# The late x work moves into light steps and the tail gets longer distances, in a graph network kernel on Trainium2

## What is computed

```python
agg = jax.ops.segment_sum(edge_attr, col, num_segments=x.shape[0])
h = jnp.concatenate([x, agg, u[batch]], axis=1)
h = jax.nn.relu(h @ W1 + b1)
out = h @ W2 + b2
x = _layernorm(x + (out + x))
```

## Time and profile before

| | us |
|---|---|
| median of 3 runs | 185.68 (185.62 to 186.27) |
| profiled execution, its own time | 185.73 |
| its span, first to last instruction | 184.0 |
| PE busy | 154.1 (84%) |
| VectorE busy | 115.4 (63%) |
| ScalarE busy | 51.5 (28%) |
| GpSimd busy | 25.4 (14%) |

### The profile page before, as it was taken

How to read it: one execution, slowest core, us unless ns; L and a number is a source line. 1 busy time by engine, 2 the same in 40 slices (tenths; PEclk the granted TensorE clock), 3 DMA queues, 4 the chain that set the end, 5 groups by cost and what they waited for, 6 DMA issues and landing times.

```text
span 184.0 us, 5378 instructions
## 1 busy us (share of the span) xinstructions
PE 154.1 (84%) x2195; PEld 113.9 (62%) x2195; DVE 115.4 (63%) x369; ACT 51.5 (28%) x110; POOL 25.4 (14%) x29
## 2 busy tenths in 40 slices
PE   0056979979979979969979999899889799899970
PEld 0046855955955956845846858467458568677850
DVE  6847499568376385485495466954933745877371
ACT  2021233223323313313313343133133241233230
POOL 7800030110200200200200204002003230000000
PEclk9999999999999999999999999999999999999997
DMA  5999999999999999999999999999999999998011
GB/s 119 315 352 373 374 375 373 371 373 374 374 374 373 375 372 373 376 372 373 374 373 374 375 373 374 375 373 360 363 374 374 371 374 370 367 398 303 11 43 33
DMA packets 42196, 62.07 MB, mean 337 GB/s; under 512 B 1975, under 2 KB 39541, under 8 KB 42170
## 3 DMA queue, kind: packets, MB, share of 16 engines
q1 hardware_dynamic: 41046, 61.23, 95.0%
q10 hardware_dynamic: 1124, 0.48, 1.2%
HBM read 58.50 MB, written 3.20 MB: 335 GB/s over the span
## 4 chain that ended last, share of the span: by engine, by line
PE 44%; DMA 39%; SPq 8%; DVE 4%; ACT 1%; issue 1%; DVEq 0%
DMA edge_ring<-in_edge_attr_dram 37%; PE sum_ps L845 17%; PE turn_ps L867 7%; PE hid_ps L907 6%; PE hid_ps L900 6%; PE out_ps L920 5%; SPq L276 4%; SPq L291 3%; DMA base_row<-in_dst_dram 2%; DVE bases L568 2%; PE xt_ps L920 1%; PE xt_ps L882 1%; DVE local_rows L576 1%; ACT local_t L429 1%; PE xt_ps L834 1%
## 5 line engine op out<-in xcount | busy, mean ns | idle before, releaser
L845 PE MATMUL sum_ps<-edge_ring,onehot 128*32 128x128 f32 x1662 | 58.5, 284 | 13.0 <-DMA edge_ring<-in_edge_attr_dram 10.8
L845 PEld LDWEIGHTS sum_ps<-edge_ring,onehot 128*32 128x32 f32 x1662 | 45.2, 113 | 27.9 <-DMA edge_ring<-in_edge_attr_dram 13.3
L630 DVE TENSOR_TENSOR agg_t<-agg_t,turn_ps 128x128 f32 x70 | 20.2, 288 | 56.7 <-PE turn_ps L867 52.6
L594 DVE TENSOR_TENSOR onehot<-iota,local_t 128x768 f32<-128x768 f32 (+1 forms) x40 | 33.6, 843 | 3.0 <-ACT local_t L429 2.4
L402 POOL TENSOR_TENSOR x_all<-x_all,half_b 128x512 f32<-128x512 f32 (+3 forms) x16 | 17.7, 1115 | 127.4 <-PE xt_ps L882 127.4
L466 ACT ACTIVATE hid_t<-hid_ps,bias 128x512 f32<-128x512 f32 (+3 forms) x32 | 18.1, 584 | 37.1 <-PE hid_ps L907 37.1
L867 PE MATMUL turn_ps<-place,sums 128*128 128x128 f32 (+1 forms) x140 | 26.5, 306 | 0.0
L907 PE MATMUL hid_ps<-agg_t,w_a 128*128 128x512 f32 (+3 forms) x64 | 24.1, 500 | 0.6 <-DVE agg_t L630 0.5
L867 PEld LDWEIGHTS turn_ps<-place,sums 128*128 128x128 f32 (+1 forms) x140 | 18.9, 192 | 8.0 <-issue 7.9
L920 PE MATMUL out_ps<-w_sb,hid_t 128*128 128x128 f32 (+1 forms) x176 | 21.9, 275 | 0.0
L441 ACT COPY sums<-sum_ps 128x256 f32<-128x256 f32 (+2 forms) x40 | 13.6, 341 | 25.9 <-PE sum_ps L845 25.9
(11 more groups left out here) (64 smaller groups left out, 73.0 us busy)
## 6 DMA issues: line engine op xcount, KB each, us to landing
edge_ring<-in_edge_attr_dram SPq DMA_DIRECT2D x69, 768.0 KB, 12.1
x_all<-in_x_dram SPq DMA_DIRECT2D x10, 256.0 KB, 10.5
out_dram<-x_all SPq DMA_DIRECT2D x1, 2304.0 KB
dst_rows<-in_dst_dram SPq DMA_DIRECT2D x1, 384.0 KB
x_all<-in_x_dram SPq DMA_DIRECT2D x1, 384.0 KB, 11.1
out_dram<-x_all SPq DMA_DIRECT2D x3, 128.0 KB
out_dram<-x_all SPq DMA_DIRECT2D x1, 256.0 KB
w_x<-in_L_gnn_W_dram ACTq DMA_DIRECT2D x1, 128.0 KB, 5.9
```

Source lines behind the costliest of these rows:

```text
L594: nc.vector.tensor_tensor(onehot[0:ROWS, b % BUFFERS, 0:k * TILES], cols, loc, ALU.is_equal).then_inc(onehot_ready, 1)
L630: nc.vector.tensor_tensor(to, to, turn_ps[b % 2][:, i * SPAN:(i + 1) * SPAN], ALU.add).then_inc(group_added, 1)
L845: last = nc.tensor.matmul(bank[c * WIN:(c + 1) * WIN], onehot[0:p, b % BUFFERS, i * TILES + c * R + r], edge_ring[0:p, slot, c * R + r], s ...
```

## The change

Node pieces: the last three are now ODD (106 nodes), E and END (128 each), so that END, a whole tile, is last. Groups 60 to 65 are handled in pairs; singles begin at group 66, which makes 37 batches. The step tables cover all pieces, and no engine has an order by hand any more. In the order of the diff:

- x of the last six pieces is loaded at groups 2, 5 and 9 (`late_load_at`) and transposed in the steps 5, 8 and 11, steps without a block's hidden or output product (`light_step`: 5, 8, 11, 14, 17, 22, 25, 28). In steps 8, 11, 14 and 17 PE multiplies the turned x of A to ODD with the x half of W1 (`sum_x_chunk`, into `out_ps`), and ScalarE keeps the result in `x_hid_late`.
- For A to ODD PE later makes the aggregate half alone, VectorE adds the kept x half (`add_x_hidden`), and ScalarE takes ReLU from the sum.
- The x half of blocks 1 to 5 and 7 to 9 is made one step earlier than the aggregate half (`hidden_x_step`).
- In the tail the output product comes two steps after the hidden one (`OUT_LATER`), the moments one step behind that, and the scaling two steps behind the moments. VectorE scales all pieces (`pool_scaled` is empty).
- `agg_t` is added first in each VectorE step; one-hot and place have five buffers and are made up to four batches ahead (`made_by`).

```diff
-BUFFERS = 3
+BUFFERS = 5
+AHEAD = 4
...
+COMPLETE_AT = [6, 12, 18, 24, 30, 36, 40, 46, 52, 58, 60, 64, 66, 67, 68]
+SINGLE0 = 66
+OUT_LATER = 2
...
+    pieces += [(odd0, odd_nodes, 1), (n_nodes - 2 * P, P, 1), (n_nodes - P, P, 1)]
...
+    hidden_step = []
+    for n in range(n_pieces):
+        at_least = hidden_step[-1] + (1 if n < ODD else 0) if n > LAST else 0
+        hidden_step.append(max(batch_first.index(complete_at[n]), at_least))
+    out_step = [b + 1 for b in hidden_step[:n_big]]
+    for n in range(A, n_pieces):
+        out_step.append(min(hidden_step[n] + OUT_LATER, n_batch + 1))
+    n_steps = n_batch + 2
+    relu_step = [h + (A <= n < E) for n, h in enumerate(hidden_step)]
+    moments_step = [o + (n >= A) + (o + (n >= A) == n_batch - 1) for n, o in enumerate(out_step)]
+    root_step = [m + 1 for m in moments_step]
+    scale_step = [m + 1 + (n >= LAST) for n, m in enumerate(moments_step)]
+    pool_scaled = range(0)
+    assert all(a <= b for a, b in zip(out_step, out_step[1:])) and hidden_step[END] == n_batch
...
+    made_by = [min(b + 3 + sum(hidden_step[n] <= b for n in range(AHEAD - 2)), n_batch) for b in range(n_batch)]
...
+    light_step = [h + 2 for h, g in zip(hidden_step, hidden_step[1:n_big]) if g > h + 2]
+    late_parts = [(A, B), (C_, ODD), (E, END)]
+    late_load_at = [2, 5, 9]
+    late_turn_step = light_step[0:3]
+    late_chunks = [(k, m) for k in range(2) for m in range(m_chunks)]
+    late_chunk_step = light_step[1:5]
+    turns = sorted([(1 if n == 0 else out_step[n - 1], (n,)) for n in range(n_big)]
+                   + list(zip(late_turn_step, late_parts)))
+    x_order = [n for _, part in turns for n in part]
+    turned_at = {part[0]: k for k, (_, part) in enumerate(turns)}
+    x_load_at = {1: 0} | {complete_at[n - 1]: n for n in range(1, n_big)}
...
+    hidden_x_step = [h - (n >= E or h - 1 in light_step) for n, h in enumerate(hidden_step)]
...
+            def add_x_hidden(n):
+                dve.wait_ge(hidden_summed, m_chunks * (n + 1))
+                if n == A:
+                    dve.wait_ge(late_x_kept, len(late_chunks))
+                for m in range(m_chunks):
+                    xh = x_hid_late[:, m, late_cols(n)]
+                    nc.vector.tensor_tensor(xh, hidden_bank(n, m), xh, ALU.add).then_inc(late_added, 1)
...
+            def scale(n):
+                norm_step(n, 3)
+                if n not in pool_scaled:
+                    norm_step(n, 4)
...
+            for b in range(n_steps):
...
+                if 0 < b <= n_batch:
                     add_batch(b - 1)
+                for n in range(A, E):
+                    if relu_step[n] == b:
+                        add_x_hidden(n)
+                if b < n_batch:
+                    for m in range(made_by[b - 1] if b > 0 else 2, made_by[b]):
+                        make_onehot(m)
+                        make_place(m - 1)
+                    if b == n_batch - AHEAD - 1:
+                        make_place(n_batch - 1)
...
+                for n in range(E):
+                    if moments_step[n] == b:
                         moments(n)
...
+                    if scale_step[n] == b:
+                        scale(n)
+            for n in range(E):
+                if moments_step[n] >= n_steps:
+                    moments(n)
+                if scale_step[n] >= n_steps:
+                    scale(n)
...
+            def sum_x_chunk(i):
+                k, m = late_chunks[i]
+                pe.wait_ge(x_t_ready, turned_at[late_parts[k][0]] + 1)
+                pe.wait_ge(y_ready, sum(b < late_chunk_step[i] for b in out_step))
+                cols = part_cols(k)
+                nc.tensor.matmul(out_ps[:, 0:cols.stop - cols.start], w1_x[:, m * P:(m + 1) * P], x_t_late[:, cols],
+                                 start=True, stop=True).then_inc(late_x_summed, 1)
...
+                alone = n_big <= n < E
+                if alone:
+                    pe.wait_ge(hidden_ready, m_chunks * n_big)
+                    if n > B:
+                        pe.wait_ge(late_added, m_chunks * (n - 1 - n_big))
...
+                for n in range(n_pieces):
                     if out_step[n] == b:
                         sum_out(n)
-                    if turn_x_step[n] == b:
-                        turn_x(n)
+                for i, chunk_step in enumerate(late_chunk_step):
+                    if chunk_step == b:
+                        sum_x_chunk(i)
+                for k, (turn_step, _) in enumerate(turns):
+                    if turn_step == b:
+                        turn_x(k)
+                for n in range(n_pieces):
+                    if hidden_x_step[n] == b and not n_big <= n < E:
+                        sum_hidden_x(n)
                     if hidden_step[n] == b:
-                        sum_hidden_x(n)
                         sum_hidden_a(n)
-                if b == late_step - 2:```

In PE's program around block 3, steps 11 to 13, there stood before (L845 sums a batch, L867 turns one, L900 and L907 are the halves of the hidden product, L920 is the output product):

```order
L845 MATMUL sum_ps<-edge_ring,onehot 32x128 x24
L867 MATMUL turn_ps<-place,sums 128x128 x2
L845 MATMUL sum_ps<-edge_ring,onehot 32x128 x24
L867 MATMUL turn_ps<-place,sums 128x128 x2
L900 MATMUL hid_ps<-x_t,w_x 128x512 x2
L907 MATMUL hid_ps<-agg_t,w_a 128x512 x2
L845 MATMUL sum_ps<-edge_ring,onehot 32x128 x24
L867 MATMUL turn_ps<-place,sums 128x128 x2
L920 MATMUL out_ps<-w_sb,hid_t 128x128 x8
```

403 lines of the change are left out of this document (180 added, 223 removed).

## The result

| | before | changed |
|---|---|---|
| median, us | 185.74 | 188.17 |
| lowest, us | 185.41 | 187.26 |
| profiled execution, us | 185.73 | 189.05 |
| its span, us | 184.0 | 187.3 |

The ratio is 1.0128 (95% interval 1.0107 to 1.0149): the changed kernel is 1.3% slower, 2.4 us by the medians. The 188.17 is the median of all six executions; the ratio leaves out one of 190.63 in the slower state, and without it the median is 187.83. Forecast was 186.3, within a range of 183.8 to 188.3. The time is in the range, near its upper end, and the forecast itself is 1.9 us too low.

The account below looks back on a forecast made before the run. Loads at 373 GB/s bound it until 144.5 us, then PE's backlog and the closing chain. Terms +1.2 - 11.8 + 9.9 - 0.7 + 0.6 - 1.0 + 1.8 + 1.1 - 0.5 = +0.6 on 185.73: 186.3 us, range 183.8 to 188.3.

Parts of the forecast that it names:

- the rival with VectorE late: Second rival: VectorE reaches the additions PE waits on late, all eight stalls grow by 0.3 us; 188.7 us, chance 0.14.
- term 3: PE stalls before the aggregate half, waiting for VectorE's additions: nine times 1.10 us with refill, +9.9 us (8.0 to 10.4).
- Term 1: Before group 7: x loads of A, B, C and ODD now stand ahead, so the interval starts later, +1.2 us.
- Term 2: After group 7: PE's 9.7 us of waits for edge loads and 2.1 us of refills go, -11.8 us.
- the 184.4 us: Time if PE loads weights ahead of the addition, so stalls have no refill; shares the faster rival's chance of 0.18.
- Terms 4 and 5: Middle of tail: B's stall goes, -0.7, A's output product waits, +0.6; groups 60 to 65 as pairs, -1.0 us.
- Term 6: Last PE steps: E's output product waits for y of C behind B's scaling, then END's work; 4.52 us, +1.8.
- Term 7: Last VectorE steps: scaling of C and ODD stands ahead of y of E and END, +1.1 us.
- Term 8: Very end: END, a whole tile, needs one store where REST needed two, -0.5 us (bounds -0.6 and 0).
- The first: First rival: loads stay the bound until group 59 and the moved work leaves the tail; 184.0 us, chance 0.18.
- The third: Third rival: loads starve behind a late PE; end as forecast or up to 1 us later, chance 0.06.

Follow-up runs that it names:

- the second set: The changed kernel run again, unchanged, beside the other experiments on one chip: 188.78 us, ratio 1.015.
- experiment 2: Changed kernel with the x half of the hidden product back in its block's own step, late x loads still early: 184.04 us, ratio 0.9896.
- experiment 4: Kernel before the change with its late x loads behind groups 2 and 9 instead of 53, nothing else moved: 185.66 us, ratio 0.9993.
- experiment 5: Kernel before the change with the x half of blocks 1 to 5 and 7 to 9 one step ahead: 185.45 us, ratio 0.9986.
- experiment 3: Changed kernel with late x loads behind groups 8, 14 and 20 and the x half in the block's own step: 184.24 us, ratio 0.991.
- the stores moved: Kernel with PE's and VectorE's tail reordered, plus E and END in one store and ODD's stores on ScalarE's queue: 181.59 us, ratio 0.9759.
- experiment 1: Changed kernel with late x loads behind groups 8, 14 and 20, late turns and chunks one such step later: 186.09 us, ratio 1.001.
- the first two kernels of experiment 7: Both edits (late loads later, x half in own step) plus E, END ahead of scaling C, ODD: 184.58 us; then also PE's order, y before scaling B: 183.19.
- scaling on POOL: Kernel with PE's and VectorE's tail reordered, plus POOL instead of VectorE scaling B, C and ODD: 182.97 us, ratio 0.9853.
- the last kernel: Kernel with the stores moved, plus B alone scaled by POOL and C scaled where VectorE waits for END's output product: 181.67 us, ratio 0.9776.

## Why the prediction was right and where it was wrong

The range held for the first set, the forecast did not hit. That the time lies in the range is partly luck: the range reaches to 188.3 because of the rival with VectorE late, and the loss that took the time there, the low clock, has no place in it; the second set, 188.78, is outside. That the estimate without the clock's loss comes to 186.1 or 186.4 is luck in part too, since it rests on errors of opposite sign: term 3 is 1.3 us too small, the other terms ahead of the last turn are together 0.6 too large, and those behind it 0.9. By the prediction's own steps:

**Term 1, +1.2: right in size, wrong in what it left out.** Group 7 starts 1.27 us later (28.00 against 26.73). The step "PE is in time for group 7 in both kernels", from which the interval was counted, hides that PE now waits for group 6 too. The last sentence of the prediction named the condition that failed: "A clock below 1.0 in the granted row would upset all terms". I had taken it as excluded because a wait of 1.7 us had left it at 1.00 in one trace, which the later traces show to be no proof: behind a wait of 1.78 to 1.82 us near 41 us the clock stayed up in three of them and fell in three. Both late loads stand ahead of group 6, and I counted their delay at group 7 without asking whether PE would wait for group 6. The missed term is +3.0 us in the profiled execution, +1.4 in the second. With the late loads ahead of group 6 the fall came near 28 us in all four profiles (the changed kernel twice, experiments 2 and 4); in the nine profiles without them it came there in none. What exactly brings the fall stays open.

**Term 2, -11.8: right in the waits.** After 28.00 there is no wait for a load. The 2.1 us of refill in it have no row of their own after.

**Term 3, +9.9: too small.** The waits are 8.8 us (0.90 seven times, 1.27 and 1.25 twice) where nine times 0.89 was 8.0. The refill is also over the 0.21: from the turn at 60.59 to the next sum at 64.11 are 3.52 us, where 0.55 for the turn and 1.81 for the aggregate half without a wait (29.79 to 31.60 in the kernel before) leave 1.16 for the stall; for C (167.02, 168.62, next sum 169.69) it is 2.67 less 0.65 and 0.86, 1.16 again. So a stall of 0.90 costs 1.16, not 1.10, and all nine 11.2 us with the two longer ones; my upper bound was 10.4. Less the clock's 3.0, the piece up to the last turn was missed by 0.7 us, while this term is 1.3 too small, so other terms ahead of it were 0.6 too high together; I cannot say which. The weight load does not run ahead of the wait: the load of w_a waits 1.09 us for the addition at 62.20. I had read the rule of the Trainium skill (TensorE: Matmul & The Clock Gate, "Step-by-step: what each phase is for"), that PE pulls weight loads ahead of matmuls in flight, as meaning no refill; that does not show here, and the 184.4 us did not come. In the kernel's program the wait on the additions (`pe.wait_ge(group_added, ...)`) stands ahead of the whole product, weight load included, so these stalls are no test of the rule itself.

**Terms 4 and 5** have no rows of their own after. For A's output product the list has no wait in the first profile (from the turn's start to the product's it is 0.84 us, where 0.65 would do) and one of 0.42 us in the second: some 0.2 and 0.6 against +0.6.

**Term 6, +1.8: right.** From the last turn's start to the end of END's product it is 5.10 us in the first profile, with that product at 1.2 GHz (1.23 instead of 0.70); at the full level it would be 4.57, forecast 4.52. The low clock there cost nothing, since VectorE was scaling C and ODD until then.

**Term 7, +1.1: 0.3 too high.** From the end of END's ReLU (181.33) to y of END (182.92) it is 1.59 us, forecast 1.9: root and handoffs took 0.21 (181.33 to 181.54), where I had 0.4.

**Term 8, -0.5: -1.1 in the profile.** From the last scaling's end to the span's end it is 3.55 us before (180.45 to 184.0) and 2.4 after. I had taken the second issue's 0.60 as the whole saving. But with this same tail five profiles have 2.4 to 3.4 us, so one profile does not size the term. Of the kernels with the tail changed, those with no store queued in front of the last have 2.3 us and those with five close together 3.35 and 3.75.

**Rivals.** The first (loads stay the bound) fell: no waits. The second (VectorE late, stalls longer by 0.3) had the right time, 188.7, for the wrong reason: of nine stalls two were longer by 0.35, one of them (block 1) by the mechanism named, VectorE at a scaling, the other (block 7) by a gap between the two additions, and taking the late loads away from groups 6 and 7 alone removed 2.1 to 2.7 us while the stalls stayed. The third could not be seen.

**What the change is made of.** The x half moved a step ahead is worth nothing while PE waits for loads (experiment 5) and is what exposes the kernel otherwise: with it back in its own step the rest of the change is 1.5 to 1.7 us faster than before (experiments 2 and 3). The early late loads cost 2 to 3 us (the later start of group 7 and the low clock together), and only together with the moved x half.

## What to carry to other kernels

Moving work out of the path of a queue that is full exchanges one wait for another; before doing it, add up how much waiting the bound leaves, because a kernel that has spent its slack has nothing left for a disturbance, and then each one reaches the end. When a transfer is put ahead of others, look at every operation that will wait, not only at the one you had in mind, and read the granted clock behind each wait in more than one execution: here TensorE's clock fell behind some waits of a length and not behind others. And when the last operations are reordered, check first that the last one really comes earlier (in one experiment here it did not), and then look at the queue that issues the stores: here that gave a further 1.6 us.

## What the runs showed of the hardware

- The granted clock fell to 1.2 GHz at two waits of PE with 0.86 us of work between them in four traces: 0.66 and 1.84, 0.73 and 1.84, 0.89 and 1.83, 1.24 and 1.84 us (the changed kernel twice, experiments 2 and 4). In a fifth with 0.66 and 1.84 it stayed at 2.4 (the stores moved, at 27.22).
- It stayed at 2.4 behind one wait of 1.74 to 2.07 us near 26.5 (experiments 1 and 5, the first two kernels of experiment 7) and behind one of 1.78, 1.78 and 1.80 near 40.7 (experiment 3, the first two kernels of experiment 7). It fell behind one of 1.80, 1.82 and 1.80 near 41 (scaling on POOL, the stores moved, and the last kernel). What tells the executions apart is open.
- How long the clock stays low differs between executions of one kernel: 1.4 or 3.0 us of loss in the changed one.
- In the tail the fall comes in some executions and not in others of nearly the same program, behind the same wait of 1.61 us: between 174 and 176 in experiments 1 and 3, not before 180 in experiment 2.
- Ahead of block 7's aggregate half the two additions of a pair on VectorE stand 0.4 us apart, in both profiles of the changed kernel and in experiment 1 (stalls of 1.25 instead of 0.90). The chain puts it down to nothing that it sees, and the cause is open:

```profile
125.93 0.30 DVE agg_t L710
...
126.31 0.41 issue
126.71 0.30 DVE agg_t L710
```

- POOL scaled a 128x128 tile in 0.78 us, VectorE in 0.30; POOL's addition of a like tile took 0.45.
